# Attention in 128-token tiles with the 513th token apart, and mixer steps placed elsewhere

## The chip, the cores and the metric

The kernel runs on one core of a Trainium2 chip. The metric is the device time of one execution in microseconds (us). TensorE is called PE, its weight loads PEld, VectorE DVE, ScalarE ACT, GpSimd POOL and SyncE SP.

## What is computed

One tower over a batch of 4 sequences, each a class token and 512 tokens of 192 channels (T = 513 rows per sequence, 2052 in all). In order: sine and cosine features and their projection; a recurrent mixer and an MLP; an attention layer with a mixture of 8 experts (2 per token); a spiking layer; an attention layer with an MLP, whose second half of the batch is weighted three ways. The parts that matter here:

```python
# mixer: proj = x @ w_in, split into gate, vraw, params (two numbers per head and token)
v  = silu(conv(vraw)); bc = (v @ w_bc); Bm, Cm = l2norm(bc[0]), l2norm(bc[1])
A, dt = softplus(p[..., 0]), sigmoid(p[..., 1]); S = 1 / (1 + dt*dt*A)
# scan over tokens:  z = S*(z - dt*A*xs + dt*B*u);  xs = xs + dt*z;  y = C . xs
# attention, twice (B = 4, 12 heads of 16 channels, 513 queries and 513 keys)
scores = einsum('bhqd,bhkd->bhqk', q, k) / sqrt(16)
attn = softmax(scores); ao = einsum('bhqk,bhkd->bqhd', attn, v)
```

## The kernel before

The tower is a row of stages, each a block in which every engine has its own written program; the order on an engine is the order of the code, and engines wait for each other by semaphores. Between two blocks all engines meet. Line numbers are those of the profile.

**Attention** (`attention`, L1886; called for both layers, "att0" and "att1"). The 513 tokens of a sequence are cut into five tiles, four of 104 and one of 97 (`KT`, L34). Work comes in 12 groups (a sequence and four heads; `gi` picks a head pair and `e` the head in it, in rows 0 to 63 or 64 to 127 of the PE array). A group takes two passes. The score pass finds each query's largest score: 20 products of one query tile with 512 keys (L1982) into a ring of three PSUM banks, each followed by a maximum on DVE (L2068); the 513th key comes from 10 two-column products (`last_keys`, L1993), joined on DVE (L2079), turned by 10 transposes (`turn`, L2004) and written as a row into the queries by ACT and DVE (`copy_max`, L1936, 513 numbers each). The second pass multiplies keys by queries (`keys`, L2027), so that the maximum is already taken off, takes the exponential on ACT (L2103, one unit is a pair of heads, a key tile and 257 queries: 104 x 514) and sums with the values (`values`, L2043, four products in four 32-column parts of the array). A group has 20 such units, in 10 steps of two. PE's order within a step is written out:

```python
for t in range(G * PAIRS + BEHIND):
    keys(2 * t); score_pair(LEAD + t); keys(2 * t + 1)
    values(2 * (t - BEHIND))
    others(LEAD + t)        # last_keys or turn, once a group each
```

`keys(n)` waits for exponential n - 2, whose banks it reuses. ACT writes out the sums of a half group (`copy_sums`, L2092) after units 3 and 13, and copies the maxima of the next group after unit 17.

**Ahead of it** (`qkv`, L1759), for each of the 20 tiles: two products into q and k (L1817, 384 columns, float32), two into v (L1822, 192 columns), a split into two halves of float16 by ACT, DVE and POOL, 12 transposes (L1839) and the copies of the turned q and k.

**The mixer's projection** (`mixer_project`, L826). PE first makes all 36 sets of parameter products (L860, 57 x 12), then 72 jobs (value and gate in turn, L868, each two float32 products of 171 columns) in a ring of six banks. DVE copies the parameters (L911) before its first job, and ACT turns them with exponential, logarithm and sigmoid (L886 to L889) before its first gate. DVE computes the lane values (L944 to L956) after job 5; PE transposes them at job 36; DVE copies the result at the end (L958). DVE's main work is the copies of the values (L933) and the convolution (L920, L923).

**The responses** (`mixer_responses`, L966). DVE fills the diagonal of a table (L1018, L1020), runs a scan over 19 steps (L1025 to L1030) and joins three parts (L1048 to L1058). PE makes 108 products (L1108), then 30 jobs of transposes of G (L1121), which ACT copies (L1095); job 8 waits for the first join and job 18 for the second. POOL clears G at the start (L1005) and another tensor near the end (L1012). Before copy 18 ACT squares the products (L1090); DVE sums the squares (L1068), ACT takes roots (L1093), DVE inverts (L1072). Last come the transposes of the end values and 8 selecting products (L1128 to L1138) and DVE's copies of them (L1074 to L1077).

**The B and C halves** (`mixer_bc`, L1147). At the end ACT casts a 57 x 3456 tensor to its high half (L1218), DVE and POOL subtract one half each (L1265, L1208), and DVE copies the high half to other rows (L1267).

## Time and profile before

| | us |
|---|---|
| median of three runs | 1756.95 |
| lowest and highest | 1753.33, 1761.33 |
| the profiled execution | 1750.74 |
| its span from first to last instruction | 1748.9 |
| PE busy | 1476.3 (84%) |
| DVE busy | 1280.7 (73%) |
| ACT busy | 1048.4 (60%) |
| POOL busy | 414.7 (24%) |
| mean granted TensorE clock | 0.905 of full speed |

The profiled execution takes 1.8 us more than its span. Busy time counts an instruction from start to end, and PE's ends are modelled, so instructions of one engine overlap, and a busy PE is not PE at its peak. In the rows, "idle before" names the work whose end let the engine go on.

### The profile page before, as it was taken

The page shows a single profiled execution, that of the slowest core. Times are in us where ns is not written, and L with a number is a line of the kernel's source. Part 1 is how long each engine was busy: PE and PEld are TensorE (multiplying, and loading weights), DVE is VectorE, ACT ScalarE, POOL GpSimd, SP SyncE. Part 2 cuts the span into 40 slices and gives each one's busy share as a digit, 9 for nine tenths or more (in the row PEclk, how much of TensorE's full clock was granted, in tenths as well). Part 3 has the DMA queues.
Part 4 walks back from the last instruction along what each step waited for, and adds up shares of the span by engine and source line. Part 5 has one row for each costly group of instructions (what it writes and reads, how often), then busy time and mean ns, then how long its engine had stood idle before and what let it go on. Part 6 is the DMA issues. An engine that isn't in the chain of part 4 may idle for free. (4 is left out here: it accounts for less than half of the span.)

```text
span 1748.9 us, 36641 instructions
## 1 busy us (share of the span) xinstructions
PE 1476.3 (84%) x14396; PEld 1114.7 (64%) x14396; DVE 1280.7 (73%) x2547; ACT 1048.4 (60%) x1871; POOL 414.7 (24%) x424
## 2 busy tenths in 40 slices
PE   5889998798499889899999719995697999999795
PEld 5889897697455657654445618895676744446574
DVE  5988897489789547369995757884655389994566
ACT  6998897334678264548896306664002549995565
POOL 0000000101656120359910117872001310000200
PEclk9999999699599989879999659998797979999897
DMA  5110100100000100025500732121100000000101
GB/s 146 28 42 29 37 1 20 36 1 1 7 2 2 35 1 15 1 82 170 171 16 2 210 119 61 61 62 50 48 1 14 1 1 2 2 2 2 35 1 37
DMA packets 52748, 67.96 MB, mean 39 GB/s; under 512 B 11535, under 2 KB 41489, under 8 KB 52578
## 3 DMA queue, kind: packets, MB, share of 16 engines
q1 hardware_dynamic: 46022, 50.30, 9.6%
q0 software_dynamic: 3840, 9.18, 1.8%
q10 hardware_dynamic: 2716, 6.14, 1.4%
q8 instruction: 115, 1.88, 0.4%
q14 instruction: 55, 0.45, 0.1%
HBM read 46.97 MB, written 18.65 MB: 38 GB/s over the span
## 5 line engine op out<-in xcount | busy, mean ns | idle before, releaser
L2068 DVE TENSOR_REDUCE att_max<-banks 104x1 f32<-104x512 f32 (+1 forms) x480 | 296.8, 684 | 10.2 <-PE banks L1982 6.5
L2103 ACT ACTIVATE att_p<-banks 104x514 f32<-104x514 f32 (+1 forms) x480 | 262.4, 599 | 31.4 <-PE banks L2027 19.1
L339 PE MATMUL banks<-tok_wT,feature_halves 128*128 128x192 f16 x2592 | 228.7, 248 | 23.9 <-DVE feature_halves L365 12.8
L339 PEld LDWEIGHTS banks<-tok_wT,feature_halves 128*128 128x128 f16 x2592 | 216.2, 99 | 33.2 <-DVE feature_halves L365 18.8
L2027 PE MATMUL banks<-att_q,att_kT 64*104 64x257 f16 (+1 forms) x960 | 157.1, 301 | 3.6 <-ACT att_p L2103 2.9
L2043 PE MATMUL banks<-att_p,att_v 104*32 104x257 f32 (+1 forms) x1920 | 154.8, 396 | 0.9
L1982 PE MATMUL banks<-att_kT,att_q 64*104 64x512 f16 (+1 forms) x480 | 126.9, 424 | 5.9 <-DVE att_max L2068 3.5
L2027 PEld LDWEIGHTS banks<-att_q,att_kT 64*104 64x104 f16 (+1 forms) x960 | 62.5, 121 | 107.0 <-ACT att_p L2103 80.4
L365 DVE TENSOR_TENSOR feature_halves<-features,feature_halves 128x2048 f16<-128x2048 f32 x54 | 123.4, 2286 | 6.5 <-ACT feature_halves L462 6.5
L134 PE MATMUL banks<-ones 128*128 128x256 f16 x654 | 88.5, 294 | 27.5 <-PEq L251 13.6
L462 ACT CAST feature_halves<-features 128x2048 f16<-128x2048 f32 x54 | 102.2, 1893 | 10.9 <-PE banks L339 10.1
L134 PEld LDWEIGHTS banks<-ones 128*128 128x128 f16 x654 | 65.7, 105 | 45.3 <-issue 25.3
L2828 ACT COPY slot_xT<-banks 128x512 f16<-128x512 f16 x40 | 23.4, 586 | 95.3 <-PE banks L2778 95.3
L740 POOL MEMSET xT<- 1x4104 f32 x1 | 3.5, 3518 | 312.6 <-POOLq L251 312.6
L1878 DVE TENSOR_TENSOR att_qkv_parts<-banks,att_qkv_parts 104x192 f16<-104x192 f32 (+1 forms) x80 | 25.1, 355 | 69.2 <-ACT att_qkv_parts L1858 69.2
L2791 PE MATMUL banks<-slot_xT,expert_w 128*128 128x128 f16 x1200 | 74.4, 221 | 0.2
L2807 PE MATMUL banks<-expert_w,slot_hidden_halves 128*128 128x192 f16 x720 | 66.1, 246 | 9.9 <-DVE slot_hidden_halves L2876 9.9
L354 DVE SCALAR_TENSOR_TENSOR angle_rest<-raw_T,freq,turns 128x1024 f32<-128x1024 f32 x54 | 69.1, 1280 | 6.2 <-ACT turns L239 5.7
L1982 PEld LDWEIGHTS banks<-att_kT,att_q 64*104 64x104 f16 (+1 forms) x480 | 51.5, 126 | 32.4 <-DVE att_max L2068 20.2
L2745 POOL DMA_INDIRECT slot_x<-token_rows,slot_comes x40 | 53.7, 1344 | 75.6 <-POOLq L2446 63.9
L2791 PEld LDWEIGHTS banks<-slot_xT,expert_w 128*128 128x128 f16 x1200 | 70.2, 99 | 1.8 <-issue 1.8
L1817 PE MATMUL banks<-att_qkv_w,xT 96*104 96x384 f32 (+3 forms) x160 | 65.0, 531 | 6.9 <-POOL att_qkv_parts L1793 4.4
(472 smaller groups left out, 3399.0 us busy)
## 6 DMA issues: line engine op xcount, KB each, us to landing
expert_w_in<-in_L_ffn_w_dram SPq DMA_DIRECT2D x16, 576.0 KB, 4.6
expert_w_halves<-expert_w_halves SPq DMA_DIRECT2D x32, 288.0 KB, 2.6
tok_w<-in_L_tok_W_dram ACTq DMA_DIRECT2D x4, 1152.0 KB, 7.2
expert_w2s<-expert_w_halves SPq DMA_DIRECT2D x1, 4608.0 KB
expert_y<-expert_out SPq DMA_DIRECT2D x6, 513.0 KB
expert_w1s<-expert_w_halves SPq DMA_DIRECT2D x2, 1536.0 KB
raw<-in_x_dram SPq DMA_DIRECT2D x2, 1152.0 KB, 5.4
expert_w1s<-expert_w_halves SPq DMA_DIRECT2D x3, 768.0 KB
```

Of the source, the lines that this page charges most:

```text
L134: pe.matmul(c.bank[bank][:, 0:256], ones[:, 0:128], ones, start=True, stop=True)
L339: ins = pe.matmul(c.bank[t // 2][:, (t % 2) * D:(t % 2 + 1) * D], fh[:, s, q, z, t * 128:(t + 1) * 128], wT[:, y, k, 6 * q + wf, :], start ...
L354: own.did(dve.scalar_tensor_tensor(fr[:, n % 2, :], rT[:, k, hf * HALF:(hf + 1) * HALF], freq_col(k, f), fm[:, n % 2, :], ALU.mult, ALU.su ...
L365: dve.tensor_tensor(fh[:, s, :, 1, :], feat[:, s, :, :], fh[:, s, :, 0, :], ALU.subtract).then_inc(flow, 1)
L462: act.copy(fh[:, s, :, 0, :], feat[:, s, :, :]).then_inc(fhigh, 1)
L1982: pe.matmul(bank_of(("s", n))[0:qn, 0:KEYS], q2[r, 2 * j + gi, b * T + q0:b * T + q0 + qn], kT[r, 2 * j + gi, b * T:b * T + KEYS], start=T ...
L2027: pe.matmul(c.pair[2 + n % 2][0:kn, 512 * e:512 * e + HALF], kT[r, 2 * j + gi, b * T + k0:b * T + k0 + kn], q2[r, 2 * j + gi, b * T + STAR ...
L2043: ins = pe.matmul(acc[32 * hh:32 * hh + 32, 0:HALF], v[0:kn, b, k, h, :], p[0:kn, (n + hh // 2) % RING, hh % 2, :], start=(k == 0), stop=( ...
L2068: dve.reduce_max(mx[0:qn, n // NS % 2, 2 * gi + e, k:k + 1], bank_of(unit)[0:qn, 0:KEYS], X).then_inc(maxed, 1)
L2103: act.activation(p[0:kn, n % RING, :, :], c.pair[2 + n % 2][0:kn, :].rearrange("p (e q) -> p e q", e=2)[:, :, 0:HALF], ACT.Exp, scale=scal ...
L2791: ins = pe.matmul(ps, ws[:, s, at:at + 128], xt[:, s, b, :], start=(k == 0), stop=(k == len(TERMS) - 1))
L2807: ins = pe.matmul(ps, hh[:, s, a, f, :], w2[:, f, b, :], start=(f == k == 0), stop=(f == NF - 1 and k == 2))
```

## The change

1. **Tiles.** Attention's queries and keys come in four tiles of 128, and the 513th token of each sequence apart. A group's score pass is 16 products and 16 maxima, one `last_queries` (4 products of the last 32 tokens with 512 keys, in four separate parts of the array, in one bank) with one maximum for it, and `last_keys` of 8 and 4 products. The second pass has per half group four steps of two units (128 x 514) and one step of a single unit for the last key: 4 products of 32 rows by 257 columns in four separate parts of one bank, an exponential of 128 x 257, and sums with a table (`vlast`) that is zero but for the last key. That makes 18 units a group in 10 steps. Steps 8 and 9 of the score side carry no pair of scores, but `last_queries` and `last_keys`. `turn` is 8 transposes and 2 products of one column, each maxima copy is a copy of 512 and one of 1 number, and ACT makes them after unit 15 (of 18) instead of unit 17 (of 20); `copy_sums` moves from unit 13 to unit 12. DVE gets a one-column maximum and one multiplication more per group.
2. **qkv** has 16 tiles of 128 and one last tile of four tokens, in which v comes from 32 products of 32 x 192 and four copies by ACT. DVE fills four pieces of `vlast` at the start.
3. **Projection.** Parameter set n is made ahead of job n, for the first 36 jobs. DVE copies the parameters at job 38, ACT turns them at job 41, DVE computes the lane values at job 54, PE transposes them at job 62. The copies that fill the table's diagonal move here, to DVE's job 70, and are gone from the start of the responses.
4. **Responses.** The transposes of the end values and the selecting products (`ends`) come ahead of job 20 instead of last, and DVE copies them before it sums the squares. ACT takes one root of ones at the start.
5. **B and C.** POOL's subtraction is gone, DVE subtracts the whole, and the copy of the high half to other rows is made straight from float32, half by DVE (before the subtraction) and half by ACT (at its end).

```diff
+AT = SEQ // 128
@@ mixer_project
-                for i in range(NBC):
...
+                def params(i):
...
                 for n, (g, m, b, s) in enumerate(jobs):
+                    if n < NBC:
+                        params(n)
...
-                    if n == len(jobs) // 2:
+                    if n == NBC + 26:
...
+                    if n == NBC + 5:
+                        lanes()
...
+                    if n == NBC + 2:
+                        dve.wait_ge(pdone, 1)
...
-                    if n == 5:
+                    if n == NBC + 18:
...
+                    if n == len(jobs) - 2:
+                        dve.wait_ge(qt, 1)
...
+                        dve.wait_ge(cleared, 1)
...
+                        own.did(dve.tensor_copy(table[:, :, :, 2:2 + (BW - 3) * (BW + 1) + 1:BW + 1], cf[:, 2:4, :, :]))
@@ mixer_responses
-            own.did(dve.tensor_copy(flat[:, :, :, 2:2 + (SUB - 1) * (BW + 1) + 1:BW + 1], cf[:, 2:4, :, :]))
...
+            act.activation(ss[:, 0:1], c.ones[0:L, 0:1], ACT.Sqrt).then_inc(squares, 1)
...
+                if n == LATE + 2:
+                    ends()
@@ mixer_bc
-            pool.tensor_tensor(half.wl[0:L, 0:MID], bwf[:, 0:MID], half.wh[0:L, 0:MID], ALU.subtract).then_inc(bwl, 1)
+            act.copy(half.wh[64:64 + L, MID:], bwf[:, MID:]).then_inc(again, 1)
+            dve.wait_ge(bwd, 2)
+            dve.tensor_copy(half.wh[64:64 + L, 0:MID], bwf[:, 0:MID]).then_inc(again, 1)
...
-            dve.tensor_tensor(half.wl[0:L, MID:], bwf[:, MID:], half.wh[0:L, MID:], ALU.subtract).then_inc(bwl, 1)
-            dve.wait_ge(bwh, 1)
-            dve.tensor_copy(half.wh[64:64 + L, :], half.wh[0:L, :]).then_inc(bwh, 1)
+            dve.tensor_tensor(half.wl[0:L, :], bwf, half.wh[0:L, :], ALU.subtract).then_inc(bwl, 1)
@@ qkv, last tile
+                        for b in range(BATCH):
+                            for hh in range(4):
+                                for o in range(2):
+                                    r = DH + o
+                                    ins = pe.matmul(c.bank[2 + b // 2][32 * hh:32 * hh + 32, b % 2 * D:(b % 2 + 1) * D],
+                                                    c.xT[0:r, o, (b + 1) * T - 32:(b + 1) * T], w[0:r, o, 2 * D:3 * D],
+                                                    start=(o == 0), stop=(o == 1))
@@ attention
+        STEPS = [[(half, k, 0), (half, k, 1)] if k < NK else [(half, k, None)] for half in range(2) for k in range(NK + 1)]
...
-                for t in range(G * PAIRS + BEHIND):
-                    if t < G * PAIRS:
-                        keys(2 * t)
-                        score_pair(LEAD + t)
-                        keys(2 * t + 1)
+                for t in range(G * NT_ + BEHIND):
+                    g, step = divmod(t, NT_)
+                    if g < G:
+                        keys(g, FIRST[step])
+                        scores(LEAD + t)
+                        if len(STEPS[step]) == 2:
+                            keys(g, FIRST[step] + 1)
                     if t >= BEHIND:
-                        values(2 * (t - BEHIND))
+                        values(t - BEHIND)
                     others(LEAD + t)
```

How it moves instructions, at three places. PE in attention, one stretch from an early step to the transposes of the next group's maxima; before (L2027 is `keys`, L1982 a score pair, L2043 `values`, L1993 `last_keys`, L2004 `turn`):

```order
L2027 MATMUL banks<-att_q,att_kT 104x257 x2
L1982 MATMUL banks<-att_kT,att_q 97x512 x2
L2027 MATMUL banks<-att_q,att_kT 104x257 x2
L2043 MATMUL banks<-att_p,att_v 32x257 x4
L1993 MATMUL banks<-att_last_keys,att_q 104x2 x10
L2027 MATMUL banks<-att_q,att_kT 104x257 x2
L1982 MATMUL banks<-att_kT,att_q 104x512 x2
L2027 MATMUL banks<-att_q,att_kT 104x257 x2
L2043 MATMUL banks<-att_p,att_v 32x257 x4
```

and the same place in the changed kernel (L2118 is `keys` for the last key, L2125 for the others, L2053 a score pair, L2143 and L2140 `values`, L2062 `last_queries`, L2075 and L2080 `last_keys`):

```order
L2118 MATMUL banks<-att_q,att_kT 32x257 x4
L2053 MATMUL banks<-att_kT,att_q 128x512 x2
L2143 MATMUL banks<-att_p,att_v 32x257 x4
L2125 MATMUL banks<-att_q,att_kT 128x257 x4
L2143 MATMUL banks<-att_p,att_v 32x257 x4
L2062 MATMUL banks<-att_kT,att_q 32x512 x4
L2125 MATMUL banks<-att_q,att_kT 128x257 x4
L2140 MATMUL banks<-att_p,att_last_values 32x257 x4
L2075 MATMUL banks<-att_last_keys,att_q 128x2 x8
L2080 MATMUL banks<-att_last_keys,att_q 32x1 x4
L2125 MATMUL banks<-att_q,att_kT 128x257 x2
```

A step with one unit has one `keys` and one `values`; two steps have no score pair between their `keys`. ACT in the first group of attention, before (L1936 the maxima copies, L2103 the exponentials, L2092 `copy_sums`):

```order
L1936 COPY att_q<-banks 1x513 x2
L2103 ACTIVATE att_p<-banks 104x514 x8
L2103 ACTIVATE att_p<-banks 97x514 x2
L2103 ACTIVATE att_p<-banks 104x514 x4
L2092 COPY att_aT<-banks 128x257
L2103 ACTIVATE att_p<-banks 104x514 x4
L1936 COPY att_q<-banks 1x513 x2
L2103 ACTIVATE att_p<-banks 97x514 x2
```

and now (L2004 and L2005 the maxima copies, L2214 the exponentials for the last key, L2217 the others, L2202 `copy_sums`):

```order
L2217 ACTIVATE att_p<-banks 128x514 x8
L2214 ACTIVATE att_p<-banks 128x257
L2217 ACTIVATE att_p<-banks 128x514 x4
L2202 COPY att_aT<-banks 128x257
L2217 ACTIVATE att_p<-banks 128x514 x3
L2004 COPY att_q<-banks 1x512
L2005 CAST att_q<-banks 1x1
L2004 COPY att_q<-banks 1x512
L2005 CAST att_q<-banks 1x1
L2217 ACTIVATE att_p<-banks 128x514
L2214 ACTIVATE att_p<-banks 128x257
```

The maxima copies now have one full and one half exponential behind them in the group, where two full ones stood. DVE at the border of projection and responses, before (the branches are the border of the blocks):

```order
L958 COPY C_start_apart<-banks 108x456
L844 UNCONDITIONAL_BRANCH
L1014 UNCONDITIONAL_BRANCH
L1018 COPY C_start_apart<-C_start_apart 108x12x19
L1020 COPY C_start_apart<-C_start_apart 108x12 x2
L1025 TENSOR_TENSOR xT<-C_start_apart 108x12x3
```

and now:

```order
L970 COPY C_start_apart<-banks 108x456
L977 COPY C_start_apart<-C_start_apart 108x12x19
L979 COPY C_start_apart<-C_start_apart 108x12 x2
L845 UNCONDITIONAL_BRANCH
L1035 UNCONDITIONAL_BRANCH
L1042 TENSOR_TENSOR xT<-C_start_apart 108x12x3
```

The table's diagonal is filled ahead of the border, and the responses begin with the scan.

## Rows read from the trace of the kernel before

**Rows 1.** Windows: length; busy PE, PEld, DVE, ACT, POOL; PEclk, DMA, GB/s.
```profile
332.30:346.30 14.00, 13.96 (x144) 13.99 (x144) 0.09 (x1) 1.28 (x1) 4.09 (x1) 0.50 0.06 12
346.30:402.30 56.00, 48.56 (x298) 47.44 (x297) 47.77 (x96) 22.44 (x54) 0.00 (x0) 0.89 0.00 1
854.20:867.90 13.70, 13.62 (x164) 6.41 (x162) 13.45 (x25) 12.38 (x25) 13.31 (x8) 1.00 0.56 171
```
**Rows 2.** Timeline of ACT over one group of attention: start, length, instruction.
```profile
853.99 0.38 ACT L2092 COPY att_aT<-banks 128x257 f32<-128x257 f32 x1
854.24 5.85 ACT L2103 ACTIVATE att_p<-banks 104x514 f32<-104x514 f32 x10
...
863.19 1.06 ACT L1936 COPY att_q<-banks 1x513 f16<-1x513 f16 x2
...
867.68 0.38 ACT L2092 COPY att_aT<-banks 128x257 f32<-128x257 f32 x1
```
**Rows 3.** Timeline of ACT in the last group, when DVE has no maxima left.
```profile
928.50 0.37 ACT L2092 COPY att_aT<-banks 128x257 f32<-128x257 f32 x1
...
942.16 0.38 ACT L2092 COPY att_aT<-banks 128x257 f32<-128x257 f32 x1
```
**Rows 4.** Timeline of PE: one step, the next one's start, last_keys and turn.
```profile
857.42 0.32 PE L2027 MATMUL banks<-att_q,att_kT 64*104 64x257 f16 x2
857.57 0.43 PE L1982 MATMUL banks<-att_kT,att_q 64*104 64x512 f16 x2
857.79 0.32 PE L2027 MATMUL banks<-att_q,att_kT 64*104 64x257 f16 x2
858.04 0.64 PE L2043 MATMUL banks<-att_p,att_v 104*32 104x257 f32 x8
858.62 0.32 PE L2027 MATMUL banks<-att_q,att_kT 64*104 64x257 f16 x2
...
859.81 0.64 PE L1993 MATMUL banks<-att_last_keys,att_q 128*104 128x2 f16 x10
...
862.75 0.63 PE L2004 MATMUL banks<-att_ident,att_max_placed 104*128 104x104 f16 x10
```
**Rows 5.** The page's part 5: busy us, mean ns; idle before, releaser.
```profile
L2068 DVE TENSOR_REDUCE att_max<-banks 104x1 f32<-104x512 f32 (+1 forms) x480 | 296.8, 684 | 10.2 <-PE banks L1982 6.5
L2103 ACT ACTIVATE att_p<-banks 104x514 f32<-104x514 f32 (+1 forms) x480 | 262.4, 599 | 31.4 <-PE banks L2027 19.1
```
**Rows 6.** Timeline of PE in qkv: the v products of two neighbouring tiles.
```profile
758.20 0.81 PE L1822 MATMUL banks<-att_qkv_w,xT 96*104 96x192 f32 x4
...
760.73 0.81 PE L1822 MATMUL banks<-att_qkv_w,xT 96*97 96x192 f32 x4
```
**Rows 7.** Timeline of the responses and the start of the B and C stage.
```profile
402.39 5.71 POOL L1005 MEMSET G<- 108x6726 f32 x1 [66.00 <-POOLq L844]
402.43 5.94 DVE L1018 COPY C_start_apart<-C_start_apart 108x228 f32<-108x228 f32 x1 [0.43 <-PEq L844]
402.43 19.66 PE L1108 MATMUL banks<-start_resp,u_T 128*57 128x96 f32 x216 [4.16 <-PEq L844]
...
425.06 8.53 PE L1121 MATMUL banks<-consts,G 108*57 108x108 f32 x72 [2.98 <-DVE G L1033]
...
442.64 4.65 POOL L1012 MEMSET C_start_apart<- 96x5472 f32 x1 [14.56 <-DVE xT L1070]
...
449.97 5.30 POOL L1201 MEMSET xT<- 32x2052 f16 x3 [2.68 <-POOLq L1002]
450.01 4.23 DVE L1245 TENSOR_TENSOR bc_normed<-bc_raw,xT 57x480 f32<-57x480 f32 x8 [0.32 <-PEq L1002]
```
**Rows 8.** Timeline of the end of the B and C stage.
```profile
471.20 1.95 DVE L1265 TENSOR_TENSOR B_end_low<-bc_raw,B_end_high 57x1728 f16<-57x1728 f32 x1 [2.28 <-ACT B_end_high L1218]
471.32 5.14 POOL L1208 TENSOR_TENSOR B_end_low<-bc_raw,B_end_high 57x1728 f16<-57x1728 f32 x1 [5.43 <-ACT B_end_high L1218]
473.19 4.19 DVE L1267 COPY B_end_high<-B_end_high 57x3456 f16<-57x3456 f16 x1
```

341 lines of the change are left out of this document (211 added, 130 removed).

## The prediction

> **What bounds the kernel now.** I read the windows first, then the timeline of one engine inside a stretch, then of its partner. In a group of attention (the last window) PE, DVE and ACT are busy 13.62, 13.45 and 12.38 of 13.70 us [rows 1]. All three look like the bound, so busy shares do not decide. The timeline of ACT gives the period: from one copy of sums at 853.99 to its like at 867.68 are 13.69 us [rows 2]. The same distance in the last group, where DVE has no maxima left and PE makes no scores, is 942.16 - 928.50 = 13.66 [rows 3]. So taking all of DVE's work away gains nothing, and what sets the period is the loop of ACT and PE. PE's timeline shows the loop [rows 4]: a step starts at 857.42 and the next at 858.62, 1.20 us, of which 0.37 are the first keys and the score pair, 0.25 the second keys (857.79 to 858.04) and 0.58 the value sums (858.04 to 858.62). ACT's ten exponentials, 0.60 long, start 0.58 apart ((5.85 - 0.6) / 9), two per step [rows 2, 5]. Ten steps are 12.0; last_keys and turn (0.64 each with their ends, about 0.57 in the queue) make 13.1; the rest, 0.6, is waiting, most of it around turn.
>
> In qkv PE does one tile after another, 2.53 us apart (760.73 - 758.20) [rows 6]. In the projection PE is busy 13.96 of the first 14.0 us with the parameters while DVE has 0.09; after that PE has 48.56 and DVE 47.77 of 56.0 [rows 1]. The granted clock is 0.50 in the first stretch, which is the lower level of 1.2 GHz, and 0.89 on average over the second, so some 12 us of it ((1 - 0.89) x 2 x 56) are still at that level and the rest at 2.4 GHz. The responses start with DVE's copy of 228 numbers, which takes 5.94 us beside POOL's memset of 5.71 [rows 7].
>
> **The change part by part.** *Attention.* Each group loses 4 of 20 maxima and gets one back, and ACT loses four full exponentials and gets two half ones. By the loop that is not what counts: it has ten steps before and after. A step of one unit costs PE 0.25 + 0.58 = 0.83 instead of 1.20, so two of them could save 0.74. The second is step 9, just behind turn. There PE waits for something else: from the start of turn at 862.75, 0.44 to ACT's first maxima copy (863.19), 1.06 for both, then one exponential (0.60), whose end the next group's first keys need: 2.1 us [rows 2, 4, 5]. ACT now makes these copies two units earlier, so one full exponential still stands between them and the next group's keys, and this chain is as long as before, while PE's own work in it is only 0.57 + 0.83. So step 9 saves nothing, and one saving of 0.37 stays. Against it: last_queries, four products of 512 columns, of which two take 0.43 in separate rows [rows 4]; if the four overlap it is 0.25, if not 0.86; I take 0.25, because the eight value records of four column parts fit in 0.64 (four of them in turn would be 1.3). ACT's two extra copies of one number lie in the chain; no row shows one so small, so between 0.02 and 0.38 (the 257-column copy) each, and I take 0.1, nearest to nothing by its size. Sum per group: -0.37 + 0.25 + 0.2 = about 0, ends -0.6 and +0.9. Once per layer there is a gain: before the first exponential DVE works through a group's maxima alone, three fewer at 0.62 (296.8 / 480) [rows 5], less 0.4 for its added small work, a guess between nothing and one maximum (0.6): -1.4. After the last maximum the drain loses a half step or two, -0.8. Rounded with some of the smaller waits, -3.5 per layer. The DVE and ACT work removed otherwise is hidden, by a loop that would run the same if it were nil.
>
> *qkv.* Four tiles fewer: -4 x 2.53 = -10.1. A tile's float32 products should not depend on its 104 or 128 rows: v takes 0.81 with 104 and with 97 [rows 6]. In the queue v takes about 0.65, q and k twice that, and the transposes the remaining 0.6, which grows by 128/104: 16 x 0.13 = +2.1. The last tile: q and k 1.3, transposes of four columns 0.5, and 32 products of 192 columns by 32. Two products of 192 take 0.65 (0.81 with the end) [rows 6]. One after another 32 would be 10.4; all in four parts at once 2.6. The order is two products into the same part, then the next part. I take 3.5, near the overlapped end, because the value sums [rows 4] also have two passes per part and overlap. Sum -2.7 per layer, ends -3.6 and +4.2.
>
> *Projection.* PE's parameters and jobs are the same work. They gain because DVE need not idle for 14 us: a job averages 48.56 / 72 = 0.67 and is about 1.15 at the lower level; five of them with their parameters (14.0 / 36 = 0.39 each) are 7.7, so the first convolution can start at about 340, ahead of even the first job of before. But DVE's own 47.8 us plus 0.9 for the table then have to fit, PE has 62.5 at the clocks of before, and ACT's detour through exponential, logarithm and sigmoid, each with a table load, now stands in the middle: its bank ring gives PE six jobs, about 3.5 us at the higher level. The first window shows a table load of 1.28 as ACT's only work; four of them and the three short activations are some 6. The clock may gain something: it stayed down through the 144 small products and rose only some time into the jobs, which now start 14 us earlier. The most is about 10 us (DVE's 48.7 behind 340, and a few us of the coupling, end at 392), the least nothing; I take -5.
>
> *Responses.* DVE's scan starts 5.7 earlier, since the diagonal is filled where POOL is idle. PE cannot use all of it: its 108 products end at 422.09 (402.43 + 19.66), and its transposes started at 425.06 after an idle of 2.98 for DVE [rows 7]. So ACT's copies, and behind them the squares, the sums and POOL's last memset, come 3.0 to 3.2 earlier: that memset ended at 447.29 (442.64 + 4.65), now 444.1. The end values are turned before it, so it is now last in the stage, which ended at 449.9: -5.8. Ends -3.0 (the tail's weave returns nothing) and -7.
>
> *B and C.* POOL's 5.14 and DVE's copy, which ended at 477.38 behind it, go; DVE has 2 x 1.95 from 471.20 to 475.1 and ACT a cast of half size behind its last copies [rows 8]: -1.5, ends -0.5 and -2.3.
>
> Sum: 2 x (-3.5 - 2.7) - 5 - 5.8 - 1.5 = -24.7. Against the profiled execution's own 1750.74 that gives 1726.0. The median of before is 1756.95, 6.2 higher, and I put the forecast there: **1732 us**. A measurement of this kernel can tell about 0.5% (8.8 us) from no change.
>
> **The rivals.** *DVE is the bound (chance 0.25).* For it speaks 13.45 busy of 13.70. Then each group loses 3 maxima at 0.62 and gains 0.5 of small work, -1.3; 13 such stretches per layer are -17 instead of -3.5: 27 less, 1705. Against it speaks the drain's 13.66 [rows 3].
>
> *The mixer keeps its time (0.18).* The scan's first multiplication would wait behind POOL's memset like the copy did, and ACT's detour in the middle would stall PE for what the start saves: the projection -0, the responses -3. That is +7.8 on the forecast: 1740. The rows speak against the first half: eight DVE products with both inputs in SBUF take 4.23 in all beside 5.30 of POOL memsets [rows 7], 0.53 each, and none is held. The Trainium skill, "SBUF — State Buffer", "Who interferes with whom", says that such an instruction contends only with a GpSimd instruction that reads SBUF, while a copy in a two-port mode contends with any; by that, the trace agrees for both.
>
> *Products in separate parts of the array do not overlap as ordered (0.07), the slower side.* Place: the 32 v products, last_queries and the one-unit keys. Price: 10.4 - 3.5 = +6.9 per layer, then per group 0.86 - 0.25 for last_queries and 0.2 for one exposed keys, 0.81 x 24 = 19.4: 13.8 + 19.4 = +33, so 1765, 0.5% above before. It decides once a group costs 0.8 more than I say; at the 0.25 taken it is nowhere. For it speaks that no row has two products into one part followed by another part, except inside the value sums.
> The Trainium skill, "TensorE: Matmul & The Clock Gate", "Part 3: Packing small matmuls — row/col tiling", says that matmuls start and end strictly in program order. By that rule the second product of a part would hold up the next part's first, half of the overlap would go, and the v products would cost 5 to 8 instead of 3.5, which makes the forecast 1735 to 1741. No row of this case shows this order.
>
> **How the numbers follow.** Forecast 0.50 (1732), DVE 0.25 (1705), mixer 0.18 (1740), no overlap 0.07 (1765). The forecast's own terms with their bounds reach from about -42 to -7, most of it between -35 and -13. Eight in ten is 1708 to 1750: it leaves out the lower part of the DVE case and the slower one. Faster by over 0.5% (below 1748.2): 0.84, the first two cases nearly whole and most of the third. Within 0.5%: 0.11. Slower: 0.05, from the last case.
>
> **What would show it.** Right: ACT's copies of sums stay 13.3 to 14.0 apart in the middle groups, with DVE busy clearly less than 13.0 of a period; ACT waits for PE before the maxima copies, longer than before; the first exponential comes 1 to 2 us earlier after the first score. The v tail of qkv takes about 3.5 from its first product to its last. The scan starts within 0.2 us of the border, and POOL's last memset ends the responses. Wrong: a period of 12.5 would mean that DVE was the bound; 14.5, that the small products do not overlap; a PE idle of over 4 us at job 47 of the projection, that the detour eats the gain; a first scan step of 5 us, that the memset holds it.

## The result and the profile after

The changed kernel takes **1768.3 us** (median of 5 runs, 1765.9 to 1772.0) against 1757.3 (5 runs of the kernel before on the same chip): a ratio of 1.0062, 95% interval 1.0038 to 1.0086. It is 0.6% slower, where 1732 was forecast and 1708 to 1750 given as the range.

The stages, each from the first product of one to the first product of the next, in the profiled executions (us; *params_first* and *one_from_bank* are kernels of the experiments below):

| stage | before | after | params_first | one_from_bank |
|---|---|---|---|---|
| projection | 70.1 | **105.7** | 73.3 | 68.9 |
| responses | 48.9 | 42.1 | 42.1 | 42.1 |
| B and C | 26.4 | 24.8 | 24.9 | 24.8 |
| chain and feed-forward | 228.0 | 227.7 | 227.8 | 227.6 |
| first qkv | 58.0 | 56.6 | 56.7 | 56.6 |
| first attention | 183.6 | 179.0 | 178.9 | 173.7 |
| experts and spikes | 402.4 | 406.7 | 407.9 | 409.8 |
| second qkv | 59.1 | 56.3 | 55.0 | 54.8 |
| second attention | 183.6 | 174.3 | 174.3 | 173.8 |
| rest | 156.5 | 158.5 | 158.3 | 158.4 |

Attention and qkv gave back 18 us, the responses with B and C 8; the projection lost 35.6. The experts and spikes and the rest, whose code is the same, were 6 longer in this trace. Windows of the changed kernel: the two stretches of before [rows 1], what the projection takes longer, and one group of attention in each layer (columns as in [rows 1]):

```profile
332.30:346.30 14.00, 13.96 (x61) 11.21 (x61) 4.19 (x9) 2.22 (x4) 4.09 (x1) 0.50 0.06 11
346.30:402.30 56.00, 56.00 (x232) 44.99 (x232) 17.68 (x33) 6.95 (x20) 0.00 (x0) 0.50 0.00 1
402.30:438.00 35.70, 26.15 (x151) 25.12 (x149) 28.00 (x59) 15.79 (x33) 0.00 (x0) 0.88 0.00 1
862.00:875.38 13.38, 13.09 (x166) 5.09 (x162) 11.88 (x26) 10.83 (x25) 12.98 (x7) 1.00 0.58 178
1490.00:1503.22 13.22, 12.99 (x165) 5.19 (x162) 11.72 (x27) 11.09 (x25) 0.00 (x0) 1.00 0.01 2
```

The second row tells it. The profile has PE busy in all of the 56.00 us, with 232 products where before had 298, and the granted clock is 0.50, its lower level of 1.2 GHz, throughout; before, it was 0.89 there. DVE, which was to be fed from the start, is busy 17.68 instead of 47.77. PE's timeline inside it (start, length, instruction, count):

```profile
334.24 0.56 PE L862 MATMUL banks<-mix_win,xT 96*57 96x12 f32 x4
334.73 1.51 PE L874 MATMUL banks<-xT,mix_win 96*128 96x171 f32 x4
336.17 0.46 PE L862 MATMUL banks<-mix_win,xT 96*57 96x12 f32 x3
```

A set and its job are 1.93 us apart (336.17 - 334.24): 1.15 for the job and 0.39 for the set, as the sums of before had it at this level, and 0.39 more where PE goes from one to the other. 36 of them are 69.5 us, and the clock rises (at 404.0) only when the last set, at 400.1, is through. A busy PE is no steady stream of columns here: with its modelled end a 171-column product stands in the profile for 0.49 us, though the next one can start 0.29 behind it, so pauses of up to 0.2 us don't show. In a row of sets at this level the 12-column products start 97 ns apart, and at the pace of the 171-column ones (286 ns) their columns would take 20 ns (an estimate).

### The profile page after: what moved, and what is told of

Read it like the earlier page. It is cut to its first block and busy times, and to the rows that moved or that the text cites. A ratio compares the mean times of both kernels' runs of the same rounds, so it can differ in the third digit from the quotient of the medians.

```text
span 1764.2 us, 36687 instructions
## 1 busy us (share of the span) xinstructions
PE 1482.6 (84%) x14444; PEld 1097.5 (62%) x14444; DVE 1235.1 (70%) x2561; ACT 1017.6 (58%) x1870; POOL 404.4 (23%) x413
## 5 line engine op out<-in xcount | busy, mean ns | idle before, releaser
L2168 DVE TENSOR_REDUCE att_max<-banks 128x1 f32<-128x512 f32 x384 | 235.0, 682 | 6.8 <-PE banks L2053 5.8
L2217 ACT ACTIVATE att_p<-banks 128x514 f32<-128x514 f32 x384 | 211.9, 600 | 31.1 <-PE banks L2125 23.0
L2143 PE MATMUL banks<-att_p,att_v 128*32 128x257 f32 x1536 | 123.5, 394 | 0.5 <-ACT att_aT L2202 0.3
L2125 PE MATMUL banks<-att_q,att_kT 64*128 64x257 f16 x768 | 112.3, 282 | 5.9 <-ACT att_p L2217 3.1
L2053 PE MATMUL banks<-att_kT,att_q 64*128 64x512 f16 x384 | 107.7, 415 | 10.2 <-PEq L1812 4.0
L135 PEld LDWEIGHTS banks<-ones 128*128 128x128 f16 x654 | 66.1, 106 | 47.2 <-issue 25.6
L2125 PEld LDWEIGHTS banks<-att_q,att_kT 64*128 64x128 f16 x768 | 36.7, 94 | 85.6 <-ACT att_p L2217 49.9
L874 PE MATMUL banks<-xT,mix_win 96*128 96x171 f32 x288 | 80.5, 442 | 5.6 <-ACT gate_silu L909 3.1
L874 PEld LDWEIGHTS banks<-xT,mix_win 96*128 96x128 f32 x288 | 64.2, 274 | 7.1 <-ACT gate_silu L909 3.3
L2921 PEld LDWEIGHTS banks<-expert_w,slot_hidden_halves 128*128 128x128 f16 x720 | 58.1, 97 | 15.1 <-issue 8.9
```

The lines of the kernel that those rows point to most:

```text
L135: pe.matmul(c.bank[bank][:, 0:256], ones[:, 0:128], ones, start=True, stop=True)
L874: ins = pe.matmul(c.bank[n % 6][:, 0:S3], w[:, o, g * DIN + m * 128:g * DIN + (m + 1) * 128], c.xT[0:DH, o, b * T + s * S3:b * T + (s + 1) ...
L2053: pe.matmul(bank_of(("s", n))[:, 0:KEYS], q2[r, 2 * j + gi, q0:q0 + 128], kT[r, 2 * j + gi, b * T:b * T + KEYS], start=True, stop=True).th ...
L2125: ins = pe.matmul(c.pair[2 + n % 2][:, 512 * e:512 * e + HALF], kT[r, 2 * j + gi, k0:k0 + 128], q2[r, 2 * j + gi, queries], start=True, st ...
L2143: ins = pe.matmul(acc[32 * hh:32 * hh + 32, 0:HALF], v[:, b, k, 4 * j + hh, :], p[:, (n + hh // 2) % RING, hh % 2, :], start=(k == 0), sto ...
L2168: dve.reduce_max(mx[:, n // NS % 2, 2 * gi + e, k:k + 1], bank_of(unit)[:, 0:KEYS], X).then_inc(maxed, 1)
```

## The experiments

**Theory.** A small set of products ahead of every job keeps TensorE's clock at its lower level for as long as the weave lasts; the rest of the change does about what was said. **Rivals.** ACT's detour and DVE's lane steps in the middle of the jobs are what costs; or the clock is low here for a reason of its own.

### The parts alone

*params_first* undoes the weave and nothing else:

```diff
-                for n, (g, m, b, s) in enumerate(jobs):
-                    if n < NBC:
-                        params(n)
+                for i in range(NBC):
+                    params(i)
+                for n, (g, m, b, s) in enumerate(jobs):
```

> The changed kernel with all 36 parameter sets ahead of the jobs again; everything else of the change stays, the late lane steps included. Theory (the weave keeps the granted clock at its lower level for as long as it lasts): the clock stands at 0.50 for the 14 us of the sets, rises some 5 us into the jobs as it did before the change, the projection takes 70 to 72 us instead of 105.7, and the kernel 1733 (1768 - 35). Rival A (ACT's detour and DVE's lane steps in the middle of the jobs are what costs): the projection keeps 90 us or more, the kernel 1752 or more. Rival B (the clock is low here for a reason ahead of the stage, not for the weave): the clock stays at 0.50 through the first 36 jobs, which alone are 41 us behind the 14 of the sets, and the kernel takes 1760 or more.

Measured 1733.4 us, ratio to before 0.9866 (0.9842 to 0.9889). *projection_alone* is the kernel before with the new mixer_project, without the fill of the table:

> The kernel before with the new projection alone (sets woven, lane steps late; the table is still filled in the responses, attention and the rest are those of before). Theory: the whole loss is here, so the projection takes about 105 us instead of 70.1 and the kernel 1792 (1757 + 35). Rival (the loss needs the other parts of the change, whose code or loads stand elsewhere): under 1775. The prediction's own step said 1752.

Measured 1789.1, ratio 1.0193 (1.0166 to 1.0221). The loss comes with the new projection (+33 on the kernel before) and goes with the weave alone (-35 on the changed kernel). Windows of 12 us in *params_first*, the first while sets and then jobs are at the lower level, the second behind the rise:

```profile
339.00:351.00 12.00, 12.00 (x97) 11.97 (x97) 0.62 (x2) 0.31 (x1) 0.00 (x0) 0.50 0.01 1
354.00:366.00 12.00, 12.00 (x84) 11.87 (x83) 11.50 (x24) 4.69 (x13) 0.00 (x0) 1.00 0.00 1
```

and the same two in the changed kernel:

```profile
339.00:351.00 12.00, 12.00 (x51) 9.64 (x51) 3.76 (x7) 0.94 (x3) 0.00 (x0) 0.50 0.01 1
354.00:366.00 12.00, 12.00 (x50) 9.64 (x50) 4.19 (x8) 1.46 (x4) 0.00 (x0) 0.50 0.00 0
```

*attention_alone* is the kernel before with AttentionTiles, qkv, attention and attention_layer of the change.

> The kernel before with attention and qkv of the change alone. The two traces compared give -1.3 and -2.8 for the two qkv stages and -4.7 and -9.3 for the two attentions, so -18: 1739. The prediction's sum for these terms was -12.4: 1745. Rival, that a group of attention is bound by DVE and gains 1.3 each (27 more): 1725 or less.

Measured 1733.7, ratio 0.9866 (0.9839 to 0.9893), some 22 us and a little more than the traces added up to; the rival that DVE sets the period would have needed 1725. *tail_bc_alone* is the kernel before with the new mixer_bc and the new mixer_responses, whose table is filled at its start as before.

> The kernel before with the end values turned sooner and the short B/C end; the diagonal of the table is filled where it was, beside POOL's memset. By the prediction's terms -5.8 + 3.0 (the start of the scan, which stays) and -1.5: -4.3, so 1753, with the first copy of the responses still 5.9 us. Rival, that nothing of it returns because something later was already waiting for another thing: 1757.

Measured 1753.1, ratio 0.9991 (0.9973 to 1.0010), which by itself is no difference. The stages of its trace show it: responses 47.2 (before 48.9), B and C 24.8 (26.4), so -3.2 of the -4.3 expected. *params_first*, which has all parts of the change but the weave, has the same ratio as *attention_alone* (0.9866 both): what the other parts give, 8 us by the stages, less the 3.2 that its projection is longer, doesn't show in the times of whole executions.

*lanes_early* is *params_first* with the lane steps back where they were: lanes() ahead of ACT's jobs, DVE's copy and maxima ahead of its jobs, its lane steps at job 5, the transposes at job 36.

> The changed kernel with all sets ahead of the jobs, as in params_first, and the lane steps of ACT, DVE and PE at the places of the kernel before; the table is still filled at the end of the projection. Theory (late lane steps cost by themselves, since ACT's four table loads stand among its gate jobs and hold the banks): the jobs take 54.5 + 0.8 us from DVE's first copy to the responses instead of 57.7, the kernel 1731 (1733.4 - 2.5). Rival (they are only moved, and DVE pays the same): 57.7, 1733.

The jobs took 55.1 us from DVE's first copy on, against 57.7. The kernel's 1732.7 (ratio 0.9886, 0.9842 to 0.9929) scatters too much to show 2.5 us; its trace ended at 1728.6 against 1732.0. The window 378.00 to 402.00 of *params_first*:

```profile
378.00:402.00 24.00, 18.90 (x108) 18.20 (x108) 19.57 (x41) 9.26 (x23) 0.00 (x0) 0.86 0.00 1
```

and of *lanes_early*, in which DVE is not kept waiting:

```profile
378.00:402.00 24.00, 20.79 (x142) 20.34 (x140) 22.93 (x46) 8.75 (x24) 0.00 (x0) 1.00 0.00 1
```

So the late lane steps cost some 2.6 by themselves, from one trace each; the same stretch of the unchanged projection took 53.2, 53.3 and 54.6 in three traces. The first rival is there, but small.

### Where the sets stand

Each kernel is the changed one with another rule for the sets, shown as the lines that replace `if n < NBC: params(n)`.

*six_at_once*:

```diff
+                    if n < NBC and n % 6 == 0:
+                        for i in range(n, n + 6):
+                            params(i)
```

> The changed kernel with six parameter sets ahead of every sixth job (0, 6, ... 30) instead of one ahead of each of 36. The work of PE is the same, but six jobs now stand in a row (7 us at the lower level, longer than the 5 us that the clock took to rise before the change). Theory 1 (what counts is the run of products of the same kind, so the clock rises inside each six jobs and falls in the sets): half of the woven stretch is at the higher level, the projection takes 75 to 90, the kernel 1740 to 1752. Theory 2 (the mixture alone counts): the clock stays at 0.50 until the last set, and only the 30 changeovers of 0.4 less are gained: 12, so projection 94, kernel 1756.

Measured 1726.7, ratio 0.9872 (0.9844 to 0.9900), better than either theory gave. Its windows:

```profile
336.00:339.00 3.00, 3.00 (x13) 3.00 (x12) 0.34 (x1) 0.34 (x2) 0.00 (x0) 0.52 0.02 0
339.00:342.00 3.00, 3.00 (x36) 2.78 (x35) 2.21 (x4) 0.60 (x2) 0.00 (x0) 1.00 0.02 5
...
366.00:369.00 3.00, 3.00 (x23) 3.00 (x22) 2.90 (x6) 1.81 (x4) 0.00 (x0) 1.00 0.00 0
```

The clock rises in the first six jobs (they begin at 334.0) and then stays up (338.9 to 376.4) for all the rows left out, through the five other runs of six sets. The products are the same and their mixture is the same as in the changed kernel; only their order differs. That the whole kernel gains by it over *params_first* isn't shown: 0.9872 against 0.9866.

*three_at_once* has `n % 3 == 0` and `range(n, n + 3)`.

> The changed kernel with three sets ahead of every third job. Theory (the clock rises only out of a run of jobs that no set interrupts for long enough; six jobs did it, 7 us at the lower level, one job never did): three jobs are 3.4 us, less than the 5 us that the clock took to rise, so it stays at 0.50 through all 36, 12 changeovers instead of 36: 57 to 60 us for the stretch, kernel about 1757. Rival (what matters is how many times PE changes between sets and jobs, in proportion): the clock is up for part of the stretch, the kernel 1735 to 1750.

Measured 1755.7, ratio 1.0028 (1.0006 to 1.0049), and the clock stayed down, as the theory said:

```profile
339.00:351.00 12.00, 12.00 (x60) 11.19 (x60) 3.77 (x7) 0.99 (x4) 0.00 (x0) 0.50 0.01 1
354.00:366.00 12.00, 12.00 (x59) 11.19 (x59) 5.15 (x10) 1.52 (x5) 0.00 (x0) 0.50 0.00 0
```

*two_from_job_18* puts two sets ahead of each of jobs 18 to 35, when the clock is up:

```diff
+                    if 18 <= n < NBC:
+                        for i in range(2 * (n - 18), 2 * (n - 17)):
+                            params(i)
```

> The changed kernel with the sets woven in twos ahead of jobs 18 to 35, so that the clock is up before the first of them. Theory (small products under the jobs pull the clock down as well as keep it down): 18 jobs in some 15 us with the clock at the higher level for most, then 0.50 again for 18 pairs at 2.3 us (1.14 job, 0.78 two sets, 0.4 changeover) = 41 us, projection 80 to 90, kernel 1742 to 1752. Rival (once up, the clock stays up, and only the start was unlucky): 18 x 1.2 = 21 us, the projection about 66, the kernel 1729.

Measured 1744.9, ratio 0.9953 (0.9936 to 0.9971). The weave begins at 344.1 with the clock at 1.00, and pulls it down:

```profile
339.00:351.00 12.00, 12.00 (x104) 10.74 (x102) 8.79 (x19) 3.23 (x9) 0.00 (x0) 1.00 0.01 1
354.00:366.00 12.00, 12.00 (x67) 10.03 (x66) 3.31 (x7) 1.30 (x4) 0.00 (x0) 0.50 0.00 1
```

*all_at_job_18* has `if n == 18:` and all 36 sets in one run.

> The changed kernel with all 36 sets in one run ahead of job 18. Theory: the clock is at 1.0 when they begin, and they take between 7.0 us (all at the higher level, half of 14.0) and 14.0 (it falls at once); one changeover only. DVE starts its copies 14 us earlier than with the sets first. Projection 62 to 70, kernel 1724 to 1732, at or under the kernel with the sets first (1733.4). Rival (any small product spoils the clock for long behind it): projection over 75, kernel over 1737.

Measured 1729.7, ratio 0.9872 (0.9855 to 0.9888); the projection took 76 us, above the 70 said and also above the 75 that the rival asked for, while the kernel's time is the theory's. The sets begin at 345.2 and the clock falls in the third us:

```profile
346.00:347.00 1.00, 1.00 (x23) 1.00 (x22) 0.95 (x2) 0.15 (x1) 0.00 (x0) 1.00 0.00 0
347.00:348.00 1.00, 1.00 (x18) 1.00 (x16) 0.96 (x2) 0.00 (x0) 0.00 (x0) 0.68 0.00 0
348.00:349.00 1.00, 1.00 (x13) 1.00 (x13) 0.34 (x1) 0.00 (x0) 0.00 (x0) 0.50 0.00 0
```

PE is busy in all of it by the profile, and the sets' products start 53 ns apart until the clock falls at 347.4. The Trainium skill, "TensorE: Matmul & The Clock Gate", "HAM oscillation — how this bites in real kernels", puts a fall of the clock down to waits in which PE stands idle between its products. No such wait is in the trace: from one product's start to the next it is at most 0.1 us in these rows and 0.45 us in the woven stretch of the changed kernel, so for this case the measurement decides against that rule as the only one. What the modelled ends leave open is how much of that time columns were moving.

*six_from_job_6* has six sets ahead of jobs 6, 12, ... 36 (`if 6 <= n <= NBC and n % 6 == 0`, sets n - 6 to n - 1).

> The changed kernel with six sets ahead of jobs 6, 12, ... 36, so that the first six jobs come first. Theory: the clock rises 5 us into the jobs, now 2.3 us earlier, and no set runs at the lower level; in six_at_once PE was busy all the time from 333 to 369 and DVE was not, so these 2 to 3 us come through: 1723 to 1725, against 1726.7. Rival (six sets pull the clock down when it has just risen, as two ahead of each job did): over 1735.

Measured 1727.3, ratio 0.9873 (0.9852 to 0.9894). The clock stayed up, but nothing came of the earlier start: DVE's first copy came 1.5 us into the stage instead of 3.9, and the jobs took 68.0 us from there instead of 64.9.

### What in a set holds the clock

*wide_beside* puts a job's products once more between each set and its job:

```diff
                         params(n)
+                        for o in range(2):
+                            pe.matmul(c.bank[6][:, 0:S3], w[:, o, 0:128], c.xT[0:DH, o, 0:S3],
+                                      start=(o == 0), stop=(o == 1))
```

> The changed kernel, and between each of the 36 sets and its job two more products of 342 columns like those of a job, whose result is not used: more work for PE, but a smaller share of it in small products. Theory (the low clock comes from how much of PE's time goes to small products with a weight load each): the clock rises inside the stretch, which takes 36 x 1.5 = 54 to 80 us in place of 69.5, and the kernel 1755 to 1775. Rival (the clock stays at 0.50 whatever stands beside the sets): 36 x 3.1 = 111 us, the kernel 1809.

Measured 1803.7, ratio 1.0286 (1.0264 to 1.0308): my theory fell, the rival holds. In its window 354 to 366, as in every other up to the last set, the clock is 0.50:

```profile
354.00:366.00 12.00, 12.00 (x49) 10.43 (x49) 0.90 (x3) 0.63 (x2) 0.00 (x0) 0.50 0.00 0
```

*long_sets* is *params_first* with long products of a set's 57 columns of weights ahead of the first 36 jobs:

```diff
+                    if n < NBC:
+                        for o in range(2):
+                            pe.matmul(c.bank[6][0:L, 0:S3], c.xT[0:DH, o, n * L:(n + 1) * L], w[:, o, 0:S3],
+                                      start=(o == 0), stop=(o == 1))
```

> params_first, and ahead of each of the first 36 jobs two more products with a set's 57 columns of weights that move 342 columns instead of 12; their result is not used. Theory A (the short passes hold the clock down: 12 columns behind each weight load): these passes are as long as a job's, so the clock rises some 5 us into the jobs and stays up; PE has 36 x 0.58 = 21 us more, of which DVE's own time covers about half, so the kernel 1738 to 1750. Theory B (the few rows and the changes of weights and bank hold it down): the clock stays at 0.50 for 36 x 2.3 = 83 us behind the 14 of the sets, the kernel 1733 + 50 = 1783 or more.

Measured 1808.5, ratio 1.0322 (1.0297 to 1.0346). Theory A fell: the passes are long, and the clock stays down for 100 us:

```profile
354.00:366.00 12.00, 12.00 (x37) 7.72 (x35) 3.43 (x6) 0.63 (x2) 0.00 (x0) 0.50 0.00 1
```

*full_sets* is *long_sets* with 128 columns of weights, `c.xT[0:DH, o, at:at + 128]` into `c.bank[6][:, 0:S3]`.

> long_sets with 128 columns of weights (of the tokens) in place of 57, so that the added products are as wide and as long as a job's and differ from it only in which tensor is the weights. Theory (57 of 128 columns of weights are what holds the clock at 0.50): it rises some 5 us into the jobs as without the added products, the kernel 1740 to 1760. Rival (the change between the two kinds holds it down, 0.42 instead of 0.29 from one pass to the next): 0.50 until the last of them, the kernel about 1808 as with long_sets.

Measured 1753.6, ratio 0.9996 (0.9979 to 1.0013), 55 us less than *long_sets* for the same count of products of the same length:

```profile
354.00:366.00 12.00, 12.00 (x85) 12.00 (x84) 6.87 (x13) 2.08 (x6) 0.00 (x0) 1.00 0.00 1
```

So it is not the change between two kinds of products. *padded_sets* gives the woven sets of the changed kernel 128 columns of weights in place of 57 (fewer in the last two):

```diff
-                        ins = pe.matmul(c.bank[7][0:L, i * 2 * SH:(i + 1) * 2 * SH],
-                                        c.xT[0:DH, o, i * L:(i + 1) * L], w[:, o, 2 * DIN:PROJ],
+                        m = min(128, NT - i * L)
+                        ins = pe.matmul(c.bank[7][0:m, i * 2 * SH:(i + 1) * 2 * SH],
+                                        c.xT[0:DH, o, i * L:i * L + m], w[:, o, 2 * DIN:PROJ],
```

> The changed kernel as it is, one set ahead of each job, but each set's weights are the 128 tokens from its first on (its own 57 and the next 71; the rows beyond 57 are not used), except for the last two, which have fewer left. Theory (the narrow weights hold the clock down): it rises inside the woven stretch, which takes 36 x 1.0 to 1.2 = 36 to 45 us plus some at the lower level in place of 69.5; the kernel 1735 to 1745. Rival (passes of 12 columns in every job hold it down as well, however wide): 0.50 until the last set, 1768.

Measured 1769.7, ratio 1.0083 (1.0051 to 1.0114), the clock at 0.50 as in the changed kernel. So the clock stood at 0.50 with weights of 57 columns under long passes (*long_sets*), and with passes of 12 columns under weights of 128 (*padded_sets*). What the two have in common isn't shown. One rival was not tried: at the lower level the passes of *full_sets* start 286 ns apart throughout, while *long_sets* has 0.47 us more per set and job where PE goes between the two widths (four of the eight distances are 449, 420, 329 and 420 ns), and a 12-column pass of *padded_sets* takes 214 ns, so pauses between products could be the cause as well as the width itself.

### Attention

*max_twice* reads the bank of the last queries' scores a second time on DVE, into a column that nobody uses.

> The changed kernel with one more reduction of 512 columns on DVE (0.61 us) in each attention group, its result not used. The prediction held that DVE has room: the groups of the second attention stay within 0.1 us of 13.22 apart, the kernel at 1768 to 1771. Rival (DVE is the bound, which would explain why the second attention gained 9.3 us and not 3.5): 13.8 apart, the kernel near 1768 + 24 x 0.6 = 1782.

A single execution gave 1769.8, and the groups of the second attention 13.22 apart, as in the changed kernel. A group of it, with DVE 0.6 us busier than above:

```profile
1498.00:1511.22 13.22, 12.98 (x167) 5.20 (x165) 12.32 (x27) 11.09 (x25) 0.00 (x0) 1.00 0.01 2
```

*copies_one_later* is *six_from_job_6* with `if i == NB - 2` for `NB - 3` at ACT's copies of the maxima.

> six_from_job_6, and in attention ACT copies the turned maxima of the next group after its exponential 16 of 0 to 17 instead of after 15. In the changed kernel ACT stands 0.78 us before these copies for PE's turn. Theory (the chain turn, two copies, exponentials, next group's first keys sets the end of the period): exponential 16 fills the wait, and only the half one stays behind the copies, so each group loses 0.3 to 0.5 and the kernel 7 to 12 (24 groups): 1713 to 1717. Rival (PE's queue sets the period, or exponential 16 waits for something that the copies free): the period stays at 13.2, the kernel within 3 us of six_from_job_6.

Measured 1728.1 (ratio 0.9868, 0.9848 to 0.9889) against 1727.3 measured beside it; groups 13.18 apart instead of 13.22. The chain from turn to the next group's first keys did not set the period.

The first attention stayed slower than the second. DVE's timeline in the changed kernel at one of its turns:

```profile
830.66 0.26 DVE L2186 TENSOR_TENSOR att_max_placed<-att_max,banks 128x8 f16<-128x8 f32 x2
830.81 0.77 DVE L2188 TENSOR_SCALAR att_max_placed<-consts,att_max_last 128x4 f16<-128x4 f32 x1
```

and POOL's beside it:

```profile
828.42 3.13 POOL L2506 TENSOR_SCALAR expert_w_in<-expert_w_in 128x1152 f32<-128x1152 f32 x1
831.62 1.14 POOL L2508 CAST expert_w_halves<-expert_w_in 128x1152 f16<-128x1152 f32 x1
```

L2188 has four numbers per partition and ends (831.58) when POOL's instruction has ended (831.55); at 815.35 it took 2.71, and 0.23 once POOL was through. L2186 beside it has an operand in a bank and takes its usual 0.18. *one_by_tensor_tensor* is *six_at_once* with tensor_tensor in place of tensor_scalar, the maxima broadcast:

> six_at_once, and in attention the maxima of the last token are placed by a product of two tensors (the maxima broadcast) instead of tensor_scalar. In the first attention of the changed kernel that tensor_scalar takes 0.77 to 2.71 us beside POOL's splitting of expert weights, against under 0.2 for its tensor_tensor neighbours, and ends when a POOL instruction ends; turn waits for it. Theory (this is why the first attention gained 4.6 us less than the second): its groups are 13.2 apart instead of 15.36 and 13.5, the first attention takes 175 instead of 178.8, the kernel 1723 (1726.7 - 4). Rival (POOL's work slows the groups in another way, its DMA or its reads): 178.8 as before, 1727.

Measured 1725.6 (ratio 0.9848, 0.9827 to 0.9869), the first attention 178.6: no gain. The instruction was still held, 1.36 at one turn, 0.83 at the first and 0.53 or 0.54 at six more, against 0.17 once POOL was through:

```profile
822.32 0.53 DVE L2189 TENSOR_TENSOR att_max_placed<-consts,att_max_last 128x4 f16<-128x4 f32 x1
```

POOL's three instructions repeat every 6.76 us (828.42 - 821.66 in the changed kernel), and the groups were 13.52 apart, twice that: the turn was locked to POOL's cycle, so a shorter hold gave nothing; behind POOL's last one they were 13.2 apart. *one_from_bank* has it read the bank, in one instruction for two:

```diff
-                        dve.tensor_tensor(mlast[:, g % 2, 1:2], mlast[:, g % 2, 0:1], bank_of(unit)[:, 4 * NK:4 * NK + 1],
-                                          ALU.max).then_inc(last_max, 1)
...
-                        dve.tensor_scalar(mexp[:, g % 2, :, NK, 32:128:64],
-                                          c.const("ident")[:, 31:128:32].rearrange("p (i e) -> p i e", e=2),
-                                          mlast[:, g % 2, 1:2], None, ALU.mult).then_inc(placed, 1)
+                        dve.scalar_tensor_tensor(mexp[:, g % 2, :, NK, 32:128:64],
+                                                 bank_of(unit)[:, 4 * NK:4 * NK + 1].unsqueeze(2).broadcast_to((128, 2, 2)),
+                                                 mlast[:, g % 2, 0:1],
+                                                 c.const("ident")[:, 31:128:32].rearrange("p (i e) -> p i e", e=2),
+                                                 ALU.max, ALU.mult).then_inc(placed, 1)
```

> six_at_once, and the maxima of the last token are placed by one scalar_tensor_tensor whose first operand is the column in the bank (the maximum with the stored one, and the product with the diagonal, in one), in place of tensor_tensor and tensor_scalar. Theory (DVE instructions whose operands all lie in SBUF wait for a POOL instruction that is under way, those that read a bank don't: the neighbours with one operand in a bank take 0.18 beside the same POOL work): the instruction takes under 0.3, the groups of the first attention are 13.2 apart instead of 13.5, the first attention takes 175 to 176 instead of 178.8, the kernel 1723. Rival (the wait falls on the first instruction behind 0.9 us of idle DVE, or on the write): it or a neighbour still takes 0.5 or more and the attention 178.6.

Measured **1724.6**, ratio 0.9838 (0.9820 to 0.9856). The first attention took 173.7 instead of the 178.8 of *six_at_once*, and its groups were 13.15 apart. That one instruction less is not what gained it shows in the second attention, where POOL has nothing to do: 173.8 against 174.2. DVE's timeline:

```profile
829.54 0.26 DVE L2185 TENSOR_TENSOR att_max_placed<-att_max,banks 128x8 f16<-128x8 f32 x2 [0.91 <-PE banks L2081]
829.69 0.23 DVE L2186 SCALAR_TENSOR_TENSOR att_max_placed<-banks,att_max_last,consts 128x4 f16<-128x4 f32 x1
```

All three observations are what the Trainium skill, "SBUF — State Buffer", "Who interferes with whom", would give: tensor_scalar can run in a mode that takes both ports and then contends with any GpSimd work, tensor_tensor with both inputs in SBUF only with work that reads SBUF, and an instruction with at most one SBUF input, outside those modes, not at all. By that, the trace agrees: 0.63 to 2.71 us, 0.53 to 1.36, and 0.23 at every turn beside the same POOL work, which reads SBUF.

The 5.2 us did not reach the end: against *six_at_once* the trace ended 0.5 sooner, with the experts and spikes at 409.8 instead of 404.4. Of these 5.4, 3.7 lie where DVE sums the experts' outputs: the loads of these began 3.8 us sooner (1196.1 against 1199.9), but DVE waited 13.3 us for them instead of 9.6. *one_from_bank* beats both kernels, as *params_first* and *six_at_once* do, and its 1724.6 is the lowest of all; whether it beats those two, which were measured at other times (0.9866 and 0.9872), isn't shown.

## Why the prediction was wrong

**The step that failed** is the projection's: "PE's parameters and jobs are the same work", and behind it "The clock may gain something". The work is the same, but its speed here was one of the order: the woven order ran at 0.50 for 69.5 us. I had the rows for it. I read that the clock "stayed down through the 144 small products and rose only some time into the jobs", and took from it that jobs which start sooner lift it sooner, without asking what sets between the jobs do. Of the 12 us that I counted at the lower level, only 5.0 (to 351.3) lay ahead of that rise; the other 6.9 (358.1 to 365.0) came with a stretch in which PE was nearly idle:

```profile
357.00:360.00 3.00, 0.47 (x2) 0.47 (x3) 2.90 (x8) 0.00 (x0) 0.00 (x0) 0.69 0.00 0
```

Both bounds of the term, 0 and -10, were on the wrong side; it measured +35.6. No rival had it either: "the mixer keeps its time" put its worst at 0. The second price that was missing is the 0.39 per set for going between a set and a job, 14 us in all at this level, which is seen in PE's timeline only once the two alternate.

The late lane steps and ACT's detour cost some 2.6 by *lanes_early*. What I wanted from the weave, DVE fed from 340 on, came only with *six_at_once*: its projection took 68.9 us with the late steps in it, 4.4 less than *params_first* but no less than the 68.7 and 68.8 that the unchanged projection took in *tail_bc_alone* and *attention_alone*. So the -5 did not come in the best order either.

**Responses and B and C: right.** Forecast -5.8 and -1.5, measured -6.7 and -1.6 by the stages. The copy of 228 numbers that took 5.94 beside POOL's memset [rows 7] is now made before it:

```profile
437.28 0.41 DVE L977 COPY C_start_apart<-C_start_apart 108x228 f32<-108x228 f32 x1
```

and the scan starts at 438.06, together with PE's first product of the stage. The last step of the B and C stage, where DVE and POOL stood before [rows 8]:

```profile
500.07 3.75 DVE L1287 TENSOR_TENSOR B_end_low<-bc_raw,B_end_high 57x3456 f16<-57x3456 f32 x1 [1.28 <-ACT B_end_high L1237]
503.09 1.62 ACT L1250 CAST B_end_high<-bc_raw 57x1728 f16<-57x1728 f32 x1
```

**qkv: right in the mechanism.** -2.7 per layer forecast, -1.4 and -2.8 measured. The v products of the last tile, two into each part of the array before the next part:

```profile
783.35 2.87 PE L1855 MATMUL banks<-att_qkv_w,xT 96*32 96x192 f32 x64
```

That is 2.8 to PE's next work at 786.15, less than my 3.5 and near the 2.6 of full overlap. The 5 to 8 that I drew from the strict order of starts and ends in the Trainium skill, "TensorE: Matmul & The Clock Gate", "Part 3: Packing small matmuls — row/col tiling", did not come; whether the products ended in order can't be seen, since the ends are modelled.

**Attention: the bound was right, its size was not.** *max_twice* shows that DVE has room, the point on which the forecast and its first rival differed. But -3.5 per layer measured -4.6 in the first and -9.3 in the second, and the groups of the second came 13.22 apart, where I had "about 0" for a group (13.70) and 13.3 to 14.0 as the sign. What failed is the count of steps: "it has ten steps before and after" let me save one half step and nothing else. PE's queue in the changed kernel, with a step of one unit (1505.48), a step without a score pair (1506.60), `last_queries` and the other step without scores (1507.83):

```profile
1505.48 0.29 PE L2118 MATMUL banks<-att_q,att_kT 64*32 64x257 f16 x4
1505.71 0.39 PE L2053 MATMUL banks<-att_kT,att_q 64*128 64x512 f16 x2
1506.03 0.64 PE L2143 MATMUL banks<-att_p,att_v 128*32 128x257 f32 x8
1506.60 0.40 PE L2125 MATMUL banks<-att_q,att_kT 64*128 64x257 f16 x4
1506.93 0.64 PE L2143 MATMUL banks<-att_p,att_v 128*32 128x257 f32 x8
1507.50 0.40 PE L2062 MATMUL banks<-att_kT,att_q 64*32 64x512 f16 x4
1507.83 0.53 PE L2125 MATMUL banks<-att_q,att_kT 64*128 64x257 f16 x4
1508.29 0.64 PE L2140 MATMUL banks<-att_p,att_last_values 128*32 128x257 f32 x8
```

From start to start in one period of the second attention, against steps of 1.21 on average before:

| | change per group, us |
|---|---|
| two steps without scores (0.90 and 1.03) | -0.5 |
| `last_queries` (0.34; 0.25 was forecast) | +0.3 |
| `last_keys` (0.58 before, 0.40 now) | -0.2 |
| six full steps (1.175 on average) | -0.2 |
| the other one-unit step (1.12; 0.83 was forecast) | -0.1 |
| the step behind turn, now of one unit too (1.70 before, 1.81 now) | +0.1 |

Without rounding these make the 0.48. The one-unit steps still have their score pair, so they save little; the two steps without scores, which I left out of the sum, bring the most. That step 9 saves nothing I had put down to the chain from turn over ACT's copies; *copies_one_later* shortened that chain and the period stayed, so what holds the step behind turn is open. For the shorter full steps and `last_keys`, the groups of weight loads, shapes apart (busy us, mean ns; idle), have a likely reason. The second attention after:

```profile
L2125 PEld LDWEIGHTS banks<-att_q,att_kT 64*128 64x128 f16 x384 | 18.3, 94 | 42.9 <-ACT att_p L2217 24.8 <-issue 8.7 <-ACT att_p L2214 5.0
```

and the first attention before:

```profile
L2027 PEld LDWEIGHTS banks<-att_q,att_kT 64*104 64x104 f16 x384 | 25.0, 122 | 45.5 <-ACT att_p L2103 34.2 <-issue 7.5
```

A load of 128 columns takes 94 ns, one of 104 takes 122. That the loads are the cause was not tried by itself. Eleven periods at 0.48 less are 5.3 of the 9.3. The rest, 4.0, is at the ends of the layer, where I had -1.4 and -0.8, rounded up to -3.5. What the first layer lacks against the second is the instruction held by POOL, an operation that I had put into "0.4 for its added small work": it costs 5.2, shown by *one_from_bank*.

**The range.** Its foot and head don't follow from the stated terms. With -0.6 and +0.9 for each of 24 groups the terms and their bounds reach from about -48 to +20, and not from -42 to -7: by its own bounds the forecast could have come out above no change. The miss did not come from there, but from the projection.

**Left open.** Why the experts and the end took 401 to 410 and 157 to 160 us from trace to trace, without a change in their code (the experts 401.2 to 403.9 in the three traces with the old attention ahead of them, 401.3 to 409.8 in the others); what it is in a set that holds the clock down, its width, its short passes or the pauses beside it; and what runs of four or five jobs would do.

## What to carry to other kernels

Before small products are woven between large ones, ask what they do to TensorE's clock: collect them in runs, ahead of all the large ones or with several large products in a row between (six did here, three did not), and look at the granted clock of the stretch, since a busy PE tells nothing of it. A small DVE instruction on the critical path can take its time from what POOL does beside it; reading one operand from PSUM freed it here. And a count of steps that stays the same says nothing when their contents change: write out the new order step by step, and price each.

## What was not expected of the hardware

- The same 144 small products and 288 of the jobs ran at 0.50 or at 1.00 by their order alone: one or three sets at a time 0.50 throughout, six at a time 1.00 from the first six jobs to behind the last set.
- PE was busy, by the profile, 56.00 of 56.00 us at the lower level of its clock, and a clock that was up fell within 3 us of a run of small products that started 53 ns apart.
- Long products with 57 columns of weights woven with the jobs left the clock at 0.50 (1808.5 us), the same with 128 columns let it rise (1753.6 us).
- Groups that waited for POOL's work took twice its cycle, 13.52 for 2 x 6.76, where they took 13.15 without the wait.
